# Moving side steps of a passage, reducing maxima over three banks, and placing up products between the last batch's steps

## What is computed

```python
x = x + tanh(g_xattn[0]) * L0_xattn(layernorm(x), ctx, ctx, mask_f)   # linear attention, 16 heads, layernorms
x = x + tanh(g_ffn[0])   * L0_ffn(layernorm(x))                       # quantised gate/up/down, 512 inner
x = x + tanh(g_xattn[1]) * L1_xattn(layernorm(x), ctx, ctx, mask_i)   # softmax attention, 16 heads of 8
x = x + tanh(g_ffn[1])   * L1_ffn(layernorm(x))                       # 8 experts, the best 2 of each row weighted
```

## Time and profile before

| | us |
|---|---|
| median of 3 runs | 733.24 (733.02 to 734.31) |
| the profiled execution: its time | 735.48 |
| its span, first to last instruction | 733.70 |
| busy in it: PE, PEld | 669.2, 471.4 |
| busy in it: DVE, ACT, POOL | 515.2, 517.9, 272.3 |
| mean granted clock of TensorE, as a share of 2.4 GHz | 0.965 |

### The profile page before, as it was taken

How to read it: one execution, slowest core, us unless ns; L and a number is a source line. 1 busy time by engine, 2 the same in 40 slices (tenths; PEclk the granted TensorE clock), 3 DMA queues, 4 the chain that set the end, 5 groups by cost and what they waited for, 6 DMA issues and landing times.

```text
span 733.7 us, 19430 instructions
## 1 busy us (share of the span) xinstructions
PE 669.2 (91%) x7326; PEld 471.4 (64%) x7339; DVE 515.2 (70%) x1250; ACT 517.9 (71%) x851; POOL 272.3 (37%) x326
## 2 busy tenths in 40 slices
PE   8899999963679999999999999999999986999997
PEld 7778888842235666566566566656666664577877
DVE  6999999979578878878888888797777741221112
ACT  7889999965247788787778777877887855624341
POOL 8799999933512322432342242143033100000000
PEclk9999999996689999999999999999999988899999
DMA  5232222534606637635654663763666370211110
GB/s 182 57 112 86 84 84 84 172 63 49 153 6 138 151 94 156 136 99 126 137 126 96 137 151 81 167 136 92 134 137 147 73 156 24 45 30 57 30 43 26
DMA packets 59667, 74.42 MB, mean 101 GB/s; under 512 B 35480, under 2 KB 40594, under 8 KB 59594
## 3 DMA queue, kind: packets, MB, share of 16 engines
q1 hardware_dynamic: 59594, 73.39, 42.4%
HBM read 32.35 MB, written 1.40 MB: 46 GB/s over the span
## 4 chain that ended last, share of the span: by engine, by line
PE 45%; DVE 16%; issue 7%; POOL 2%; ACT 2%; SPq 1%; another core or an unknown queue 1%; DMA 1%; DVEq 0%; POOLq 0%; ACTq 0%
DVE mx L1721 8%; PE ps L690 8%; PE ps L778 7%; PE ps L851 7%; PE ps L839 7%; PE ps L765 6%; PE ps L676 4%; PE ps L682 2%; DVE kvall L1552 2%; PE ps L712 1%; DVE amax L1591 1%; POOL KP L1204 1%; DVE silu L1636 1%; DMA QS<-QD 1%
## 5 line engine op out<-in xcount | busy, mean ns | idle before, releaser
L1087 ACT ACTIVATE P<-ps,kbias,kscale 125x896 f32<-125x896 f32 x192 | 210.7, 1098 | 88.9 <-PE ps L765 85.5
L1721 DVE TENSOR_REDUCE mx<-ps 128x1 f32<-128x500 f32 x336 | 214.3, 672 | 47.9 <-PE ps L690 46.2
L690 PE MATMUL ps<-KP,Qb 128*128 128x500 bf16 x336 | 129.2, 387 | 16.4 <-DVE mx L1721 10.3
L1204 POOL TENSOR_TENSOR KP<-kvall,KP 128x1500 bf16<-128x1500 f32 x16 | 48.6, 3038 | 231.1 <-ACT KP L1030 231.1
L778 PE MATMUL ps<-P,Vp 125*32 125x112 f32 x3072 | 115.4, 268 | 2.3 <-ACT O L1095 0.9
L778 PEld LDWEIGHTS ps<-P,Vp 125*32 125x32 f32 x3072 | 68.4, 110 | 52.9 <-issue 38.4
L540 PE MATMUL ps<-wkv,cT 128*125 128x256 f32 x384 | 91.4, 381 | 0.2 <-ACT arena L950 0.2
L540 PEld LDWEIGHTS ps<-wkv,cT 128*125 128x125 f32 x384 | 68.8, 189 | 9.1 <-issue 0.4
L1148 ACT ACTIVATE arena<-ps,b 128x448 f32<-128x448 f32 x64 | 40.5, 634 | 47.3 <-PE ps L839 41.4
L765 PE MATMUL ps<-QS,KS 128*128 128x112 bf16 x768 | 69.1, 215 | 2.4 <-DVE QS L1727 1.4
L765 PEld LDWEIGHTS ps<-QS,KS 128*128 128x128 bf16 x768 | 55.3, 99 | 23.5 <-issue 4.2
(11 more groups left out here) (219 smaller groups left out, 1022.2 us busy)
## 6 DMA issues: line engine op xcount, KB each, us to landing
cT<-ctxT_dram SPq DMA_DIRECT2D x31, 750.0 KB, 4.1
KS<-KP SPq DMA_DIRECT2D x48, 375.0 KB, 7.2
arena<-KP SPq DMA_DIRECT2D x48, 375.0 KB, 7.3
QS<-QD SPq DMA_DIRECT2D x96, 28.0 KB, 5.5
wgu<-w_dram SPq DMA_DIRECT2D x8, 256.0 KB, 3.1
silu<-w_dram SPq DMA_DIRECT2D x8, 256.0 KB, 3.1
x<-xh_dram SPq DMA_DIRECT2D x1, 512.0 KB, 4.7
cT<-ctxT_dram SPq DMA_DIRECT2D x1, 500.0 KB, 4.4
```

The source lines that it names most:

```text
L690: ins = nc.tensor.matmul(ps[:, bank, 0:KCW], q[:, 128 * c:128 * c + 128], KP[par][0][:, KCW * k:KCW * k + KCW], start=True, stop=True)
L1087: nc.scalar.activation(P[t % 2][0:TK, :].rearrange("p (k n) -> p k n", k=2), src, ACT.Exp, scale=kscale[0:TK, bass.ds(n, 1)], bias=kbias[0 ...
L1204: nc.gpsimd.tensor_tensor(KP[par][2][:], krest, KP[par][1][:], ALU.subtract).then_inc(sem("kp3_ready"), 1)
L1721: ins = v.tensor_reduce(mx[:, c, k:k + 1], ps[:, bank, 0:KCW], AX.X, ALU.max)
```

## The change

1. K2 stands behind AT and DE in TensorE's and ScalarE's programs and in EARLY_SIDE behind AT.0. VectorE's rounding of the gate and up weights moves behind the dense sums, down_weights behind hidden_quantised, add_beta behind `normed`, and output_bias and masks between the two query_parts.
2. The maxima of batch 0 are no units any more. `first_maxima(c)` writes a chunk's three products into banks 0 to 2 (even c) or 3 to 5 (odd c), and VectorE reduces the three banks with one instruction. K0', K1' and K2' come after chunks 1, 3 and 5. GpSimd writes Qb for batch 0 in two instructions, heads 0 to 4 and 5 to 15; chunks 0 and 1 wait only for the first.
3. The logits go to bank 4, and expert 0's up units 0 to 3 and the logit tiles 0 to 6 stand between OT, FT, FO and ET. The units of all experts are numbered with k outside, so units 0 to 3 read the first half of the batches.

```diff
-EARLY_SIDE = ["K0", "K1", "K2", "AT.0", "V0", "V1", "G.0", "U.1", "V2", "HT.0", "HT.1", "LT.0", "Q1.0", "K0'", "K1'",
+EARLY_SIDE = ["K0", "K1", "AT.0", "K2", "V0", "V1", "G.0", "U.1", "V2", "HT.0", "HT.1", "LT.0", "Q1.0", "K0'", "K1'",
...
-EARLY_AUX = [..., "LT.1", "Q1.1"] + MXS + ["SH"]
-KEYS_AMONG = {"MX3": "K0'", "MX9": "K1'", "MX15": "K2'"}
+EARLY_AUX = [..., "LT.1", "Q1.1", "SH"]
+KEYS_AMONG = {1: "K0'", 3: "K1'", 5: "K2'"}
...
+            def first_maxima(c):
+                if c == 0:
+                    pe.wait_ge(sem("qb_begun"), 1)
+                    pe.wait_ge(sem("kp1_ready"), KC)
+                if c == 2:
+                    pe.wait_ge(sem("qb_ready"), 1)
+                if c == 1:
+                    for unit in ("LT.1", "Q1.1"):
+                        pe.wait_ge(sem(free_of(BEFORE, unit)), emptied(BEFORE, unit))
+                if c > 1:
+                    pe.wait_ge(sem("mx_taken"), c - 1)
+                q = Qb[0][:].rearrange("p h s -> p (h s)")
+                for k in range(KC):
+                    ins = nc.tensor.matmul(ps[:, KC * (c % 2) + k, 0:KCW], q[:, 128 * c:128 * c + 128],
+                                           KP[0][0][:, KCW * k:KCW * k + KCW], start=True, stop=True)
+                ins.then_inc(sem("mx_ready"), 1)
...
-            fill(BEFORE, "K2", 0, 0)
             pe.wait_ge(sem("att0_ready"), 2)
             both("AT", "DE")
-            for unit in ("V0", "V1"):
+            for unit in ("K2", "V0", "V1"):
                 fill(BEFORE, unit, 0, 0)
...
-            for unit in MXS + ["SH"]:
-                fill(BEFORE, unit, 0, 0)
-                if unit in KEYS_AMONG:
-                    fill(BEFORE, KEYS_AMONG[unit], 1, 1)
+            for c in range(CH):
+                first_maxima(c)
+                if c in KEYS_AMONG:
+                    fill(BEFORE, KEYS_AMONG[c], 1, 1)
+            fill(BEFORE, "SH", 0, 0)
...
+            pe.wait_ge(sem("side_free"), emptied((NT - 1, 1), "ET"))
+            up(0, 0, True, range(0, 1))
             fill(AFTER, "OT", B - 1, 1)
-            for unit in LAST:
-                fill(AFTER, unit, NT - 1, 1)
+            up(0, 0, True, range(1, 2))
+            fill(AFTER, "FT", NT - 1, 1)
+            logits(range(0, 3))
+            fill(AFTER, "FO", NT - 1, 1)
+            up(0, 0, True, range(2, 4))
+            logits(range(3, NT - 1))
+            fill(AFTER, "ET", NT - 1, 1)
             pe.wait_ge(sem("side_free"), emptied(AFTER, "ET"))
...
+            logits(range(NT - 1, NT)).then_inc(sem("logit_ps"), 1)
...
-            up(0, 0, True)
+            up(0, 0, True, range(4, 8))
...
-                    c, k = divmod(u, 2)
+                    k, c = divmod(u, FC)
...
             pool.wait_ge(sem("qp0_ready"), 1)
-            masked(0, 0)
+            masked(0, 0, 0, 5, "qb_begun")
+            masked(0, 0, 5, H)
...
+            for c in range(CH):
+                dve.wait_ge(sem("mx_ready"), c + 1)
+                v.tensor_reduce(mx[:, c, :], ps[:, KC * (c % 2):KC * (c % 2) + KC, 0:KCW], AX.X,
+                                ALU.max).then_inc(sem("mx_taken"), 1)
+            dve.wait_ge(sem("mx_taken"), CH)
+            v.tensor_reduce(mneg[:], mx[:], AX.X, ALU.max, negate=True).then_inc(sem("mneg_ready"), 1)
+            empty(BEFORE, "SH", 0, 0)
```

More of the change, by code:

```diff
@@ L818, in _, with up @@
             weigh(B - 1, 1, T - 1, False)
-            fill(AFTER, "OT", B - 1, 1)
-            for unit in LAST:
-                fill(AFTER, unit, NT - 1, 1)
-            pe.wait_ge(sem("side_free"), emptied(AFTER, "ET"))
[L825 to L840, removed]
+            def up(e, par, first, of=range(8)):
+                xv = xT[:].rearrange("p (b q) -> p b q", q=HALF)
+                for u in of:
+                    k, c = divmod(u, FC)
+                    if u == 0:
+                        pe.wait_ge(sem(f"w1_in{par}"), loads(e, par))
+                    if not (first and u < 4):
+                        pe.wait_ge(sem("h_ready"), 8 * e + u - 3)
+                    nc.tensor.matmul(ps[:, u % 4, 0:8 * S], w1_sb[par][:, 128 * c:128 * c + 128],
+                                     xv[:, 8 * k:8 * k + 8, 0:S], start=True, stop=True).then_inc(sem("up_ps"), 1)
@@ new lines, in logits @@
+            def logits(tiles):
+                for t in tiles:
+                    ins = nc.tensor.matmul(ps[:, 4, E * t:E * t + E], xT[:, 128 * t:128 * t + 128], gw_sb[:],
+                                           start=True, stop=True)
+                return ins
+            pe.wait_ge(sem("side_free"), emptied((NT - 1, 1), "ET"))
+            up(0, 0, True, range(0, 1))
+            fill(AFTER, "OT", B - 1, 1)
+            up(0, 0, True, range(1, 2))
+            fill(AFTER, "FT", NT - 1, 1)
@@ L847, in down @@
                         pe.wait_ge(sem("moe_done"), 2 * e + k - 3)
+                    elif par == 0 and k == 0:
+                        pe.wait_ge(sem("logit_ready"), 1)
                     for t in range(min(4, ND - 4 * k)):
@@ L1060, in _ @@
             act.wait_ge(sem("filled"), 1)
-            for unit in EARLY_SIDE[0:3]:
+            for unit in ("K0", "K1"):
                 key_part1(BEFORE, unit, 0, 0)
             both("AT")
+            key_part1(BEFORE, "K2", 0, 0)
             act.wait_ge(sem("nd_ready"), 2)
@@ L1213, in parts, with masked @@
                                         ALU.subtract).then_inc(sem("qp_ready"), 1)
-            def masked(par, n):
+            def masked(par, n, lo=0, hi=H, done="qb_ready"):
                 z = slot(n)
-                nc.gpsimd.tensor_tensor(Qb[par][:], bc(QP[0][:, z, HALF * par:HALF * par + S], 1, [128, H, S]),
-                                        bc(hmask1[:], 2, [128, H, S]), ALU.mult).then_inc(sem("qb_ready"), 1)
+                nc.gpsimd.tensor_tensor(Qb[par][:, lo:hi, :],
+                                        bc(QP[0][:, z, HALF * par:HALF * par + S], 1, [128, hi - lo, S]),
+                                        bc(hmask1[:, lo:hi], 2, [128, hi - lo, S]), ALU.mult).then_inc(sem(done), 1)
             def queries(b, par, n, at):
                 if at is not None:
-                    pool.wait_ge(sem("aux_ready"), filled(at, MXS[-1]))
+                    if fixed(at[0]) and at[0] < 0:
+                        pool.wait_ge(sem("mx_ready"), CH)
+                    else:
+                        pool.wait_ge(sem("aux_ready"), filled(at, MXS[-1]))
                     pool.wait_ge(sem(f"stacked{par}"), loads(b - 2, par, 2 * STACK))
@@ L1514, in _, with up_weights @@
             v.tensor_scalar(wg2[:, 1:2], wg2[:, 0:1], wmean[:, 1:2], None, ALU.mult)
-            step(v.tensor_scalar(wgu[:], wgu[:], ROUND, -1.0, ALU.subtract, ALU.max))
-            v.tensor_scalar(wgub[:], wgu[:], 1.0, None, ALU.min).then_inc(sem("wq_ready"), 1)
+            def up_weights():
+                step(v.tensor_scalar(wgu[:], wgu[:], ROUND, -1.0, ALU.subtract, ALU.max))
+                v.tensor_scalar(wgub[:], wgu[:], 1.0, None, ALU.min).then_inc(sem("wq_ready"), 1)
             def masks():
@@ L1686, in _ @@
                 dense(BEFORE, n)
-            add_beta(2, NT)
+            up_weights()
             for n in range(2):
                 first_sum(n)
-            masks()
             for n in range(2):
@@ L1704, in _ @@
                 hidden_quantised(n)
-            output_bias()
+            down_weights()
             for n in range(2):
@@ L1709, in _ @@
                 normed(n)
-            for n in range(2):
-                query_parts(BEFORE, n)
+            add_beta(2, NT)
+            query_parts(BEFORE, 0)
+            output_bias()
+            masks()
+            query_parts(BEFORE, 1)
             def empty(at, unit, b, par):
```

10 lines of the change are left out of this document (3 added, 7 removed).

## The result

The changed kernel takes 726.48 us (median of 6 runs, 725.05 to 726.89), the kernel before in the same sessions 734.96 (733.02 to 736.96). The ratio is 0.9879, 95% interval 0.9862 to 0.9897: 8.9 us faster, where I forecast 7.9. The time itself is 1.2 us above the 725.3 that I gave, chiefly because I had counted from a median of three runs of the kernel before (733.24), and six give 734.96. The profiled execution took 725.42 with a span of 723.6, 10.1 us under the span before.

What follows compares the result with a forecast made beforehand. The chain through the passage's engine steps and VectorE's maxima, then TensorE at the end, bounds the kernel. Passage 5.2 plus end 2.7 gives 7.9 us, so 725.3 from the median 733.24; range 724.0 to 727.5 (58%).

Steps and rivals of the forecast that it cites:

- Passage, step 1: Passage to cross attention, VectorE's side steps moved and K2 behind AT and DE: gate starts 2.7 us earlier, about 174.5.
- 0.4 without cover: Before the gate: ScalarE's later turned-query eviction costs nothing under VectorE's three key_rest steps (1.8 us); without them 0.4 us.
- the others delay only query part 1, to 190.2: Passage: output bias and masks (0.6, 0.7 us) delay only query part 1, from 189.4 to some 189.8, done at 190.2.
- Step 2 and 3: Passage: split mask brings little beyond the side steps; three-bank maxima take 12.4 us against 15.0, 2.6 us gained.
- rival for "slower": Maxima's seven three-bank reduces are dear: from 3.0 us each they eat both gains and 1.5 more; 4%.
- The wait behind K0': In the maxima: one wait of 0.85 us behind this key part, and none once the clock is up.
- Passage together: Passage to cross attention: 2.7 + 2.6, less 0.1 for a shift product that may meet the half clock, 5.2 us.
- End: Kernel end, up products moved into waits: 5.3 us at held clock, less 2.6 (2.0 to 3.7) for half clock: 2.7.
- the rival of a later load: Kernel end: table load does not start right behind the exp, so the end saves 1.7 us, total 726.3; 8%.
- The rival that the clock holds: Kernel end: granted clock stays up through the gelu wait, the end gains 5.3 us, total 722.7; 15%.
- Windows as a block: Between passage and end: the eight window pairs wait only for each other and shift as a block.

Runs made afterwards that it cites:

- a2_after: The changed kernel profiled and timed once more, unaltered: 725.64 us, ratio 0.9880 to the kernel before.
- e4_warm: Changed kernel with 11 idle fp32 products before the fifth up product, where TensorE waits for the gelu: 723.79 us, ratio 0.9847.
- e6_banks: Changed kernel with expert 0's up units 4 to 7 in banks 5, 7, 6 and 4, not waiting for earlier gelus: 721.52 us, ratio 0.9826.
- e5_masks: Changed kernel with output bias and masks moved from between the query parts to behind the second wide reduce: 727.54 us, ratio 0.9898.
- e9_place: e6_banks with output bias in the down product's wait, masks behind the last maxima reduce; output_bias overwrites bmask before add_beta reads it: 721.16 us.
- e3_max: Kernel before with only the split mask and one reduce over three banks per chunk of the maxima: 731.64 us, ratio 0.9956.

## Why the prediction was right, point by point

- **Passage, step 1** (2.7 us to the gate): 2.5 in the first pair of profiles, and 3.2 and 3.6 where the clocks are alike up to there (22.1 to 18.9 and 23.1 to 19.6 us after K0). AT could start 1.9 earlier and did; the mixed rows were there. With the clock up in both profiles the dense sums gained 1.55 for my 1.45, the weights' rounding cost 0.3 and not 0.6, and the masks gave 0.7 and not 0.5. ScalarE was late for the gate in the first profile of the changed kernel, which I had costed at nothing: VectorE stood for 0.41 us, because TensorE's K2 met the half clock (mean 0.66 in 162 to 164) and took 1.58 us. In the second K2 took 1.00 and the gate didn't wait. So the cover that I had counted on was enough at full clock, and that the 0.41 is the size of my "0.4 without cover" is luck.
- **The step that was mis-sized: "the others delay only query part 1, to 190.2".** It was done at 191.3 (192.43 less 1.10). I had taken output bias and masks at 1.3 us from rows where GpSimd stood still; here they lie on GpSimd's masked queries, and took 2.5. The scaling of the bias, 0.29 us before, took 1.15, the scale of the masks 0.52 instead of 0.23, while the step that reads PSUM kept its 0.29. It looks like waiting, not like sharing: the scaling ended 0.09 us after GpSimd's second instruction of masked queries did (191.06 and 190.97), and 0.08 after it in a2_after, e4_warm and e6_banks; the step L1560, which began between two instructions of GpSimd, kept its 0.25. The Trainium skill (GPSIMD Engine Reference, Specifications) says that GpSimd's SBUF interfaces are shared with VectorE, with contention for VectorE's two-port modes or two SBUF inputs; the trace agrees. e5_masks and e9_place confirm the size: 1.1 us on the first reduce, each against the profile of the changed kernel with the same clock.
- **Step 2 and 3** (2.6 us): 2.4 in the first pair of profiles and 3.2 in the second (15.3 to 12.1). The reduce's price of 1.72 from the line through two rows was exact, and so PSUM across three banks costs nothing of its own; that was the rival for "slower", and it falls. The wait behind K0' was 1.12 us in one profile and 0.49 in the other, for my 0.85, but it hung on the late second query part as well as on the half clock: e3_max, with the half clock and chunk 1 on time, hasn't got it.
- Passage together: 5.2 forecast, 4.1 and 6.7 in the two pairs, 5.4 with the clock alike at 162 to 168 us. This is partly luck: the gate came 0.5 to 0.9 earlier than I had it, and the late second query part took 0.8 back before the first reduce. The 1.1 us by which the first reduce differs in the two profiles of the kernel before (38.0 and 39.0 us after K0) are the dense sums' wait for TensorE at the half clock, 1.22 us.
- **End** (2.7 us): 3.3 and, in the second pair, 2.8. ET 0.39 late for my 0.4, the wait 2.81 for my 2.7, the load 0.02 us behind the exp (617.75 to 617.77), so the rival of a later load falls. The Trainium skill (ScalarE: Activation LUTs, What ACT_TABLE_LOAD costs) has a drain of 1.38 us beside the load, and this row shows none; the measurement decides. The clock fell as forecast, but the half clock cost 1.95 us against my price of a product at full clock (1.7 against e4_warm) instead of 2.6: 2.0 was my lower end.
- **The rival that the clock holds** did not happen, but e4_warm shows what it was worth: 1.7 us.
- **Windows as a block**: right as far as the second pair of profiles shows (403.9 and 404.3), not in the first. 406.1 against 402.3 would have looked like a gain of the change if it hadn't been repeated.
- Sum: 7.9 forecast, 8.9 measured (7.6 to 10.1 by the interval). The forecast lies within the interval. Passage and end give 5.4 and 2.8 to 3.3, so 8.2 to 8.7; the rest is less than the clock's falls move from one profile to the next.

## What to carry to other kernels

Price a new wait by what it does to the clock too. Here a gap of 2.8 us on TensorE cost its own length and 1.7 us of half clock behind it; useless products in the gap got back the second, and free banks, which removed most of the gap, got back both (3.5 us). A side step is only free in an idle stretch of its own engine where GpSimd isn't writing SBUF as well, and where TensorE doesn't stand still for it. And before a gain is put down to an edit, look whether it lies in a stretch that the edit touched, profile both kernels twice, and compare a stretch only between profiles whose granted clock is alike in it.

## What I had not expected of the hardware

Two profiles of one program differ by 2 us in the length of the windows (406.1 and 403.9, 402.3 and 404.3), by how long the granted clock is down at two places where TensorE idles 2.8 us or less; in the passage a fall that comes some 8 us earlier or later moves the first reduce by 1.1 us. The fall comes after the idle time: in the last window before, TensorE resumed at 598.2, the fall is in the stretch from 598 to 600, and full clock comes back in the stretch from 606 to 608; in the second profile of the same kernel it was back by 602. A table load started 0.02 us behind the last activation (617.75 to 617.77). A step of VectorE of 0.29 us took 1.15 beside GpSimd and ended 0.09 us after GpSimd's instruction.
